# Two cross attentions and a coupled attention: heads' scores in pairs, softmax sums from a column of ones, one copy in another place

## The reference, cut to what matters

```python
q = x @ W_q + b_q;  k, v = ctx @ W_k + b_k, ctx @ W_v + b_v      # ctx: [16, 375, 256]
scores = einsum('bhqd,bhkd->bhqk', q, k) / sqrt(16)              # masked
A = softmax(scores, axis=-1)
x = layernorm(x + (einsum('bhqk,bhkd->bhqd', A, v) @ W_o + b_o))
```

## Time and profile before

| | |
|---|---|
| median of three executions | 2441.42 us |
| profiled execution, its own time | 2437.63 us |
| span of its records | 2435.9 us |
| PE, DVE, ACT, POOL busy | 90%, 71%, 54%, 21% of the span |
| granted TensorE clock, mean | 0.96 |
| cross0, first to last head's scores | 140.8 us to 483.2 us |
| coupled | columns' copies at 965.5 to 1156.5 us |
| cross1, first to last head's scores | 1192.2 us to 1535.0 us |

### The profile page before, as it was taken

The page is one execution under the profiler, slowest core; times in us unless marked ns, Lnnn a source line. Parts: engine busy times, 40 slices in busy tenths (PEclk is TensorE's granted clock), DMA queues, the critical chain, the costliest instruction groups (busy, mean ns, idle before and its releaser), DMA issues. The chain is left out here.

```text
span 2435.9 us, 48613 instructions
## 1 busy us (share of the span) xinstructions
PE 2197.9 (90%) x15771; PEld 1853.4 (76%) x15771; DVE 1724.2 (71%) x4286; ACT 1319.0 (54%) x3188; POOL 513.9 (21%) x421
## 2 busy tenths in 40 slices
PE   8789999859999976898799999799999999999995
PEld 5578777747999965565678777678888888888884
DVE  2567777755888854777477778687776777768564
ACT  3257777744666634656477777444444444444441
POOL 3200000010111052322100000023333333333333
PEclk9889999979999997999799999899999999999997
DMA  4067666322766621000456666122322323222222
GB/s 116 3 147 137 130 126 128 80 75 90 230 200 210 186 67 37 1 0 0 118 129 139 130 129 138 56 80 84 106 93 95 106 77 113 88 97 93 70 76 68
DMA packets 201755, 246.50 MB, mean 101 GB/s; under 512 B 58481, under 2 KB 176706, under 8 KB 201602
## 3 DMA queue, kind: packets, MB, share of 16 engines
q1 hardware_dynamic: 198050, 235.37, 36.8%
q0 software_dynamic: 3552, 9.18, 1.3%
HBM read 202.95 MB, written 41.55 MB: 100 GB/s over the span
## 5 line engine op out<-in xcount | busy, mean ns | idle before, releaser
L843 ACT ACTIVATE cross_pr<-cross_sc,cross_mn 112x375 f32<-112x375 f32 x512 | 311.6, 609 | 188.9 <-DVE cross_mn L939 180.7
L2389 POOL TENSOR_TENSOR switch_gl<-switch_gb,switch_gh 128x896 fp32r<-128x896 f32 x128 | 270.9, 2117 | 572.9 <-ACT switch_gh L2570 572.9
L939 DVE CUSTOM_DVE_ANT_0 cross_sc<-cross_ps,cross_masked 112x375 f32<-112x375 f32 x512 | 272.9, 544 | 86.8 <-PE cross_ps L728 74.9
L736 PE MATMUL cross_ps<-all_ident,cross_pr 112*125 112x112 f32 x1536 | 255.7, 275 | 30.0 <-DVE cross_pt L946 28.7
L2626 DVE SCALAR_TENSOR_TENSOR switch_vt<-switch_ps,switch_chosen,switch_vt 112x128 f32<-112x128 f32 x512 | 144.1, 344 | 189.4 <-PE switch_ps L106 184.7
L736 PEld LDWEIGHTS cross_ps<-all_ident,cross_pr 112*125 112x125 f32 x1536 | 232.4, 189 | 51.1 <-DVE cross_pt L946 32.3
L728 PE MATMUL cross_ps<-cross_k,cross_q 96*112 96x376 f32 x512 | 214.7, 420 | 15.4 <-DMA cross_k<-cross_k_dram 11.7
L104 PE MATMUL switch_ps<-switch_vw,switchgates_xh 128*112 128x512 f32 x512 | 209.3, 409 | 4.9 <-ACT switch_vt L2549 4.9
L104 PE MATMUL switch_ps<-switch_gh,switch_ow 128*128 128x448 f32 x512 | 192.5, 376 | 18.0 <-POOL switch_gl L2389 16.7
L106 PE MATMUL switch_ps<-switch_vw,switchgates_xl 128*112 128x512 f32 x512 | 202.5, 395 | 0.0
L105 PE MATMUL switch_ps<-switch_vw,switchgates_xh 128*112 128x512 f32 x512 | 202.0, 395 | 0.0
(11 more groups left out here) (397 smaller groups left out, 5734.7 us busy)
## 6 DMA issues: line engine op xcount, KB each, us to landing
switch_gb<-switch_gt_rows SPq DMA_DIRECT2D x128, 448.0 KB, 3.6
experts_w_raw<-in_L_ffn_w_dram SPq DMA_DIRECT2D x42, 1024.0 KB, 5.6
cross_k<-cross_k_dram SPq DMA_DIRECT2D x96, 375.0 KB, 7.8
cross_k_dram<-cross_ks SPq DMA_DIRECT2D x32, 750.0 KB, 4.7
all_place<-in_ctx_dram SPq DMA_DIRECT2D x32, 375.0 KB
cross_q<-cross_q_dram SPq DMA_DIRECT2D x192, 56.0 KB, 4.4
all_place<-in_L_ffn_v_w_dram SPq DMA_DIRECT2D x16, 512.0 KB, 6.2
all_place<-in_L_ffn_o_w_dram SPq DMA_DIRECT2D x8, 1024.0 KB, 7.2
```

The costliest lines, as they stand in the source:

```text
L736: last = nc.tensor.transpose(ps[0:KP, TURNED + h % 2, t * T:(t + 1) * T], pr[:, h % NB, t * KP:(t + 1) * KP], ident[0:T, 0:T])
L843: nc.scalar.activation(pr[:, h % NB, :], sc[:, h % NB, :], ACT.Exp, bias=mn[parity][:, h:h + 1], scale=-1.0, accum_out=rs[parity][:, h:h + ...
L939: nc.vector.tensor_tensor_reduce(out=sc[:, h % NB, :], in0=ps[0:T, SCORES + h % 2, 0:S2], in1=mask_of[:], scale=-0.25, scalar=3e38, op0=AL ...
L2389: pool.tensor_tensor(gl[u % 2][:], gb[u % RING][:], gh[u % 2][:].bitcast(F32), ALU.subtract)\
```

## The change

In the cross attentions PE's `scores` is called at every second step and makes two heads' scores in a row. Its wait is for the maximum of the head directly before the pair. A unit V or K stands directly behind the pair, in front of the transposes; C0, C1 and Q stand behind them and move to steps 7, 9 and 11. ACT takes its units at steps 8, 10, 12, 13, 15 instead of 7, 8, 10, 12, 14, DVE its eight units at odd steps, V0 and V1 at 5, K0 and K1 at 15. The exponent no longer sums: the values tile gets ones in column 16 of each head's 32, the sum comes out of the product with the values, and the reciprocal reads it from PSUM. In the coupled attention `copy_columns` is put in front of the tanh.

```diff
-        rs = [s.sb(f"rs{b}", [T, H]) for b in range(2)]
...
+            c = Chain(pool, pool_chain)
             for b in range(2):
-                last = pool.memset(vv[b][:], 0.0)
+                c.link(pool.memset(vv[b][:], 0.0))
+                last = pool.memset(vv[b][:, :, :, HD:HD + 1], 1.0)
...
-                wait(pe, s_max, b * H + h - 1)
-                nc.tensor.matmul(ps[0:T, SCORES + h % 2, 0:KEYS], q[parity][:, h // 2, h % 2, :],
-                                 kk[parity][:, h // 2, :], start=True, stop=True).then_inc(s_done, 1)
+                wait(pe, s_max, b * H + h)
+                for n in (h, h + 1):
+                    nc.tensor.matmul(ps[0:T, SCORES + n % 2, 0:KEYS], q[parity][:, n // 2, n % 2, :],
+                                     kk[parity][:, n // 2, :], start=True, stop=True).then_inc(s_done, 1)
...
-            FRONT_AT = {2: V0, 4: V1, 6: V2, 7: C0, 8: C1, 10: Q, 12: K0, 14: K1}
+            FRONT_AT = {2: V0, 4: V1, 6: V2, 7: C0, 9: C1, 11: Q, 12: K0, 14: K1}
...
-                    scores(b, parity, i)
+                    if i % 2 == 0:
+                        scores(b, parity, i)
+                    u = FRONT_AT.get(i)
+                    if u in units and u not in (C0, C1, Q):
+                        front(b + 1, 1 - parity if u in (V0, V1, V2) else parity, u)
...
-                                     scale=-1.0, accum_out=rs[parity][:, h:h + 1]).then_inc(exped, 1)
+                                     scale=-1.0).then_inc(exped, 1)
...
-            FRONT_AT = {7: C0, 8: C1, 10: Q, 12: K0, 14: K1}
+            FRONT_AT = {8: C0, 10: C1, 12: Q, 13: K0, 15: K1}
...
-                    dve.wait_ge(exped, b * H + H)
-                    ch.link(nc.vector.reciprocal(ri[:], rs[parity][:]))
                     dve.wait_ge(t1_done, b + 1)
+                    turned = ps[0:T, TAIL, :].rearrange("p (h e) -> p h e", e=32)
+                    ch.link(nc.vector.reciprocal(ri[:], turned[:, :, HD]))
...
-            FRONT_AT = {4: V0, 5: V1, 6: V2, 8: C0, 9: C1, 11: Q, 13: K0, 15: K1}
+            FRONT_AT = {5: (V0, V1), 7: (V2,), 9: (C0,), 11: (C1,), 13: (Q,), 15: (K0, K1)}
...
                 exponent(b, 1)
+                if before:
+                    copy_columns(b - 1)
                 if not last:
                     tanh(b + 1, 1 - parity)
-                if before:
-                    copy_columns(b - 1)
```

More of the change, by code:

```diff
@@ L490, in stage_cross_attention @@
         xn_ready, xt_done, xt_ready, chain = (s.sem(n) for n in ("xn_ready", "xt_done", "xt_ready", "chain"))
+        pool_chain = s.sem("pool_chain")
         CHAIN = 5
@@ L787, in batch @@
                         turn(b - 1, i - TL + H)
-                    if FRONT_AT.get(i) in units:
-                        u = FRONT_AT[i]
-                        front(b + 1, 1 - parity if u in (V0, V1, V2) else parity, u)
+                    if u in units and u in (C0, C1, Q):
+                        front(b + 1, parity, u)
                     if not first and i in TAIL_AT:
@@ L949, in tail @@
                 if part == 0:
-                    dve.wait_ge(exped, b * H + H)
-                    ch.link(nc.vector.reciprocal(ri[:], rs[parity][:]))
                     dve.wait_ge(t1_done, b + 1)
-                    nc.vector.tensor_tensor(otok[:], ps[0:T, TAIL, :].rearrange("p (h e) -> p h e", e=32)[:, :, 0:HD],
+                    turned = ps[0:T, TAIL, :].rearrange("p (h e) -> p h e", e=32)
+                    ch.link(nc.vector.reciprocal(ri[:], turned[:, :, HD]))
+                    nc.vector.tensor_tensor(otok[:], turned[:, :, 0:HD],
                                             ri[:].unsqueeze(2).broadcast_to([T, H, HD]), ALU.mult).then_inc(otok_ready, 1)
@@ L976, in batch @@
                     maximum(b, parity, i)
-                    if FRONT_AT.get(i) in units:
-                        u = FRONT_AT[i]
-                        front(b + 1, 1 - parity if u in (V0, V1, V2) else parity, u)
+                    for u in FRONT_AT.get(i, ()):
+                        if u in units:
+                            front(b + 1, 1 - parity if u in (V0, V1, V2) else parity, u)
                     if not first and i in TAIL_AT:
```

## The result

The changed kernel takes 2480.49 us (median of 4 executions, 2468.22 to 2483.68) against 2440.77 us (2438.83 to 2442.55) of the kernel before on the same chip: ratio 1.0154, 95% interval 1.0118 to 1.0189. It is 40 us slower, where 12 us faster was forecast. The profiled execution took 2479.22 us, its span is 2477.2 (before: 2437.63 and 2435.9), its mean granted clock 0.945 (before 0.960).

What follows compares the result with a forecast made beforehand. No engine is full, so order of work and waits set the period. Cross stages gain 17 us, coupled loses 4.7: −12, to 2429 us by the median; own range 2420 to 2437, 8 in 10 from 2410 to 2447.

Steps and rivals of the forecast that it cites:

- cross batches otherwise: Cross batches with all projection units: 21.8 us for 22.17, 0.35 gained per batch, 9 us in 26 batches.
- last two intervals of each stage: Last two batches of each cross stage, with fewer or no units: 3.9 us gained per stage, between 1 and 4.
- coupled, first to last copy of columns: Coupled stage: 13 batches each 0.43 us longer, 5.6 lost; batch 1 gains 0.9; net loss 4.7 us.
- the walk: Cross batch followed step by step through PE, DVE and ACT with distances from the old timeline: 21.8 us for 22.17.
- the two waits: PE in a cross batch: idle about 0.8 us before the second key unit, over 1 us before head 14's transposes.
- The first half: Cross batch, first score of heads 2 and 3 to head 12's maximum: 14.0 us for 15.8, gain 1.8.
- the second half: Cross batch, head 12's maximum to the next batch's scores of heads 2 and 3: 7.80 us for 6.37, loss 1.43.
- PE was the bound: Rival, cross stages: all 1.0 us of PE work saved per batch arrives, 26 us, total 2413; chance 0.10.
- Slower, through the query unit: Rival, head 12's maximum to the next pair: from 8.5 us on it decides; period 22.9, total 2459; chance 0.18.
- its 0.43: Coupled batch: tanh starts 0.43 us later behind the columns' copy, lengthening the chain over POOL to the normalised rows.
- the ones as a gain: Cross attentions: no accumulator reading, 0.1 us less per exponential on ACT, 0.5 per batch, already part of the 0.35.
- the gain of 0.43 per cross batch: Cross batch: estimate by the rule that a change of tiling mode drains TensorE, 0.43 us shorter instead of 0.35.

Runs made afterwards that it cites:

- Experiment 5: Experiment 2 with five unread filler products on PE in front of head 14's transposes: 2438.25 us, ratio 1.001 to the kernel before.
- experiment 6: Experiment 2 with the second key unit behind head 11's transposes on PE instead of in front: 2415.54 us, ratio 0.9913 to the kernel before.
- 7: Experiment 6 with ACT taking the second key unit at step 14 instead of 15: 2404.9 us, ratio 0.9871 to the kernel before.
- Experiment 2: The changed kernel with the coupled stage's columns' copy back behind the tanh, cross edits kept: 2473.75 us, ratio 1.0143 to the kernel before.

## Why the prediction was wrong

The forecast was −12 us; the profiled executions differ by +41.6. By terms, each from the intervals of the two traces:

| term | forecast | measured |
|---|---|---|
| low clock, 21 batches × 1.5 | 0 | +31.5 |
| cross batches otherwise, 26 (22 × 0.15, then 0.26 and 0.61 twice) | −9.1 | +5.0 |
| last two intervals of each stage, by the division's product | −7.8 | −6.5 |
| coupled, first to last copy of columns | +4.7 | +4.4 |
| in front of the first division of cross0 and of cross1 | 0 | +2.4, +4.0 |
| between the stages and behind cross1 | 0 | +0.6 |
| sum | −12 | +41 |

*The failed step* is the sentence "I take the walk, whose steps are all distances of this timeline". All these had been read at a granted clock of 1.00, and the sum carries them over to a loop with new waits; a lower clock has no term in it and no rival. What the runs showed in its place is 21 batches of 26 with 3.4 us at half the clock, 1.5 us each, 31.5 us. The walk itself produced the two waits, 0.8 us in front of K1 and over 1 in front of T of 14, and the last part even named them as signs. It priced them by what they delayed and not by the clock behind them. Experiment 5 shows that price apart from everything else: 10 small instructions in the place of the wait, 32 us back. Experiments 6 and 7 agree with real work: with the waits shortened to 0.35 and 0.56, or to 0.35 and none, no batch is low.

*The first half was mis-sized*, the second term of the error. At full clock it took 14.4 us from the pair to M of 12 (282.37 to 296.76) where the walk said 14.0, and the second half 7.93 for 7.80. With that the period at full clock is 22.3, 0.15 over before instead of 0.35 under, 14 us over both stages. Most of it has arrived when the tail's four transposes start, 5.88 us after the pair and not 5.54 (the walk's 6.14 less their own 0.60): two T behind an fp32r unit cost 0.63 (305.84 to 306.47) and not 0.50, and the small rest is spread. The walk also adds 6.14 and 1.05 to 7.3 where they make 7.2, so by its own steps it was 0.1 more optimistic than it wrote. Its remark that 13 batches of a stage repeat to 0.1 us holds for 11 of the 13 intervals; the other two took 21.98 and 21.48. Even without the clock the cross edits would have made the kernel no faster: experiment 5, ratio 1.001.

*A term put at nothing*: the sum has no first batch. From its first maximum to that of the next batch it takes 21.8 us in cross0 and 22.1 in cross1 for 19.9 before. That is most of the +2.4 in front of the first division of cross0. In cross1 a 22nd low stretch (granted clock 0.50 from 1236.1 to 1239.5) lies there too, another 1.5 us of the +4.0.

*The rivals.* "PE was the bound" is refuted for the whole batch, right for the first half: that is why the clock could hurt. "Slower, through the query unit" had the right place and sign, but its condition, a second half of 8.5 us or more, did not occur; the 7.93 here are nearly the walk's. None of them was the clock, and the range, built from them, could not reach 2480.

*What was right*: the wait moved in the coupled stage and its 0.43 (0.41). That its whole term came out (+4.4 for +4.7) is partly luck: the first batch gained 2.6 and not 0.9, and the last but one lost 2.1 that the sum did not have. Right were also the places of DVE's idle times and roughly their lengths (0.56, 0.56, 0.69 and 1.45 for 0.75, 0.75, 0.8 and 1.3); none at K0; a gain at the ends, if not its size (the last two intervals, reckoned by the division's product, by 3.2 per stage for 3.9); the ones as a gain; nothing for the reciprocal from PSUM (0.25 in both); and the step from T to the values' product, 0.41 again (295.91 to 296.32). For the gain of 0.43 per cross batch that the prediction gives beside this step no working is shown, and no run shows it.

*What stays open.* Five batches of cross0 kept the full clock; in the one shown the waits are the same to 0.01 us. The clock records show a pattern. In a run of long batches the low stretches begin 23.89 us apart, while a long batch takes 23.82, so each begins a little later behind T of 14: in cross0 2.0, 2.1, 2.2 and 2.3 us behind it, then in two batches none, then 2.1, 2.2, 2.2 and 2.3 and again none. Experiment 2 repeats this. In cross1 they begin 0.8 to 1.7 us behind it, in every batch from the first on. So it seems to go with where the waits lie in time and not with how long they are. No run shifts them to test this, and why it should be so is open. Executions of the changed kernel differ by 15 us, which ten low batches more or less would make; the mean clocks of the two that differ by this, 0.950 and 0.943, fit that number.

## What to carry to other kernels

A wait on TensorE can have two prices: its length, and the clock behind it, which here fell due in the TensorE-bound stretch that came next. When a walk through a new order produces a wait of about 1 us on TensorE that was not there before, and above all several close together, make a rival of "the next stretch runs at half the clock" and price it from rows at the lower level; then look for the unit whose wait can be moved behind ready work, which was worth 2.3% here (experiment 6 against 2). A unit in front of the transposes is no gain where it has to wait for its bank: it then holds the transposes behind it, and moving it behind them took a full-clock batch from 22.3 to 21.5 us.

## What the hardware showed that was not expected

- A loop in which TensorE is idle for about 2.4 us of 22.3, in waits of at most 1.2 us, loses the full clock once a round, in 21 rounds of 26, for 3.4 us each. Each costs 1.5 us of 22.3.
- Work that nobody needs can make a kernel faster: 1.33 us of filler per batch brought 1.3%. It pays only while it fits the wait: 2.89 us of it brought nothing.
- DVE's normalisation beside POOL's masking took 1.75 us again (0.40 in the cross stage) and ended 0.14 after the masking's second part (1104.87 + 1.68). The same is seen with the copy in its old place in the prediction's rows (1.76 us, 0.15 after).
